# A DLRM tower on one core: the dot products of a tile issued in two parts instead of one

## The reference

```
e = stack([tbl_f[ids[:, f]] for f in range(27)], axis=1)     # [2048, 27, 128]
dot = einsum('bnd,bmd->bnm', e, e)
z = the 351 entries of dot with n < m, per sample
h = concatenate([z, dense_ctx], axis=1)                      # [2048, 367]
h = maximum(h @ W_top1 + b_top1, 0)                          # 512
h = maximum(h @ W_top2 + b_top2, 0)                          # 256
y = h @ W_top3                                               # [2048, 1]
```

## Time and profile before

| | before |
|---|---|
| runs, us | 588.22, 588.62, 590.11 |
| the profiled execution, us | 590.46 |
| its span, first to last instruction, us | 588.6 |
| mean granted TensorE clock, share of 2.4 GHz | 0.794 |
| TensorE matmul busy, us | 399.7 (68%) |
| GpSimd busy, us | 270.0 (46%) |
| VectorE busy, us | 248.6 (42%) |
| ScalarE busy, us | 163.6 (28%) |
| DMA, GB/s over the span | 62 |

### The profile page before, as it was taken

How to read it: one execution, slowest core, us unless ns; L and a number is a source line. 1 busy time by engine, 2 the same in 40 slices (tenths; PEclk the granted TensorE clock), 3 DMA queues, 4 the chain that set the end, 5 groups by cost and what they waited for, 6 DMA issues and landing times.

```text
span 588.6 us, 13981 instructions
## 1 busy us (share of the span) xinstructions
PE 399.7 (68%) x6083; PEld 360.4 (61%) x6083; DVE 248.6 (42%) x770; ACT 163.6 (28%) x217; POOL 270.0 (46%) x286
## 2 busy tenths in 40 slices
PE   4520176657595876949687685948778487969776
PEld 3420156557484775838586574938667476959665
DVE  5500224636244462506544262625635163647112
ACT  3210223314233222412324031422223132334241
POOL 6777462627446252645526164453536264530000
PEclk9855586958588686968879597887878697989898
DMA  8932130445213121321213022221213122210000
GB/s 196 246 87 59 35 79 20 111 126 139 55 46 72 29 72 29 71 52 50 68 30 82 22 64 57 51 73 29 73 38 77 34 55 69 54 34 2 2 2 2
DMA packets 23004, 36.65 MB, mean 62 GB/s; under 512 B 6224, under 2 KB 17120, under 8 KB 22944
## 3 DMA queue, kind: packets, MB, share of 16 engines
q0 software_dynamic: 8896, 18.24, 12.8%
q1 hardware_dynamic: 14048, 17.52, 11.8%
HBM read 35.73 MB, written 0.01 MB: 61 GB/s over the span
## 4 chain that ended last, share of the span: by engine, by line
PE 61%; issue 19%; another core or an unknown queue 9%; ACT 5%; DVE 2%; DMA 2%; SPq 1%; ACTq 0%; DVEq 0%
PE embT_ps L371 29%; PE gram_ps L397 12%; PE h_ps L426 7%; PE h_ps L450 5%; PE embT_ps L381 4%; ACT embT L575 2%; PE flat_ps L409 2%; PE embT_ps L366 2%; DMA embT<-in_tbl 2%; ACT embT L567 2%; DVE one_hot L493 2%; ACT tbl L555 1%; SPq L290 1%; SPq L282 0%
## 5 line engine op out<-in xcount | busy, mean ns | idle before, releaser
L340 POOL DMA_INDIRECT emb<-in_tbl,idx x272 | 263.5, 969 | 249.5 <-PE embT_ps L381 153.8
L371 PE MATMUL embT_ps<-one_hot,tbl 125*128 125x256 f32 x1284 | 214.1, 328 | 52.7 <-DVE one_hot L493 28.2
L493 DVE TENSOR_SCALAR one_hot<-ids,row_of 125x256 fp32r<-125x256 int32 x658 | 197.3, 371 | 108.9 <-PE embT_ps L371 47.9
L371 PEld LDWEIGHTS embT_ps<-one_hot,tbl 125*128 125x128 f32 x1284 | 195.5, 228 | 62.7 <-issue 30.7
L397 PE MATMUL gram_ps<-embT 128*27 128x27 f32 x4096 | 72.8, 217 | 97.5 <-issue 90.0
L397 PEld LDWEIGHTS gram_ps<-embT 128*27 128x27 f32 x4096 | 58.5, 129 | 113.4 <-issue 104.1
L567 ACT COPY embT<-embT_ps 128x256 f32<-128x256 f32 x77 | 52.1, 677 | 227.6 <-PE embT_ps L371 161.7
L575 ACT COPY embT<-embT_ps 128x512 f32<-128x512 f32 (+1 forms) x80 | 87.0, 1091 | 19.9 <-PE embT_ps L381 10.9
L521 DVE STREAM_TRANSPOSE flat<-gram_ps 128x864 f32<-128x864 f32 x16 | 17.3, 1083 | 169.2 <-PE gram_ps L397 169.2
L381 PE MATMUL embT_ps<-ident,emb 128*128 128x128 f32 x272 | 46.5, 288 | 29.8 <-ACT embT L567 22.4
L381 PEld LDWEIGHTS embT_ps<-ident,emb 128*128 128x128 f32 x272 | 34.3, 149 | 31.5 <-issue 31.0
(11 more groups left out here) (38 smaller groups left out, 75.1 us busy)
## 6 DMA issues: line engine op xcount, KB each, us to landing
ids<-in_ids_hot SPq DMA_DIRECT2D x77, 128.0 KB
emb<-in_tbl,idx POOLq DMA_INDIRECT x272
embT<-in_tbl SPq DMA_DIRECT2D x5, 448.0 KB
w_sb<-in_tbl SPq DMA_DIRECT2D x3, 560.0 KB
w_sb<-in_W_ring SPq DMA_DIRECT2D x1, 756.0 KB
w_sb<-in_W_top SPq DMA_DIRECT2D x1, 512.0 KB
h1T<-in_tbl SPq DMA_DIRECT2D x1, 448.0 KB
w_sb<-in_tbl SPq DMA_DIRECT2D x1, 448.0 KB
```

The lines of the kernel that those rows point to most:

```text
L340: pool.indirect_dma_start(gathered_row(t, s), None, tables[f][:, :], bass.IndirectOffsetOnAxis(ap=idx[:, t, f:f + 1], axis=0),).then_inc(g ...
L371: mm = pe.matmul(out[:, 0:HN], tbl[0:ROWS, part, AT[o] + chunk, :], one_hot[0:ROWS, k % SLOTS, c, :], start=(chunk == 0 and part == 0), st ...
L493: done = dve.tensor_scalar(one_hot[0:ROWS, k % SLOTS, c, :], of, row_of[0:ROWS, KINDS.index(CH[o]), chunk:chunk + 1], None, ALU.is_equal)
```

## The change

The dots of tile t - 1 are issued as two steps in a middle tile: groups 0 to 15 (64 samples) behind quad 0, where all were, and groups 16 to 31 behind quad 2. In the last tile the second part stands behind quad 0 of that tile, with a layer one between the parts. For the dots of the last tile itself, a layer two stands between the parts. VectorE's fill goes where the second part is.

```diff
@@ plan(t)
-            dots = [[("dots", t - 1, 0, GROUPS32)]]
+            dots = [[("dots", t - 1, 0, GROUPS32 // 2)], [], [("dots", t - 1, GROUPS32 // 2, GROUPS32)]]
...
-            return [("flat", t - 2), *dots[0], ("layer1", t - 3), ("quad", t, 0), ("layer1", t - 2),
+            return [("flat", t - 2), *dots[0], ("layer1", t - 3), ("quad", t, 0), *dots[2], ("layer1", t - 2),
                     ("quad", t, 1), ("layer2", t - 3), ("quad", t, 2), ("ring", t - 1), ("flat", t - 1),
                     ("layer2", t - 2), ("quad", t, 3), ("layer1", t - 1), ("quad", t, 4)]
...
-    END = [("dots", T - 1, 0, GROUPS32), ("layer2", T - 2), ("ring", T - 1), ("flat", T - 1), ("layer1", T - 1),
+    END = [("dots", T - 1, 0, GROUPS32 // 2), ("layer2", T - 2), ("dots", T - 1, GROUPS32 // 2, GROUPS32), ("ring", T - 1), ("flat", T - 1), ("layer1", T - 1),
            ("layer2", T - 1)]
```

## The result

| | before | after |
|---|---|---|
| runs, us | 588.22, 588.62, 590.11, 596.67 | 631.61, 632.13, 632.84, 636.47 |
| median, us | 589.37 | 632.49 |
| span of the profiled execution, us | 588.6 | 629.8 |
| mean granted clock | 0.794 | 0.805 |

The ratio is 1.0717, 95% interval 1.0618 to 1.0815: slower by 43 us, where 626 us was forecast, +37 on the median of before. That is the answer for the chip on which both ran. On another chip the same two kernels came out the other way round (0.9286), and what goes with that is the main thing that the experiments found.

A forecast was written before the change was run, and what follows sets the result against it. Gathers being issued on GpSimd were taken to slow TensorE's dots. Terms 3.6 + 1.3 - 1.8 = +3.1 us per tile, x 13 = +40, less 2.4 at the last tile, gave 626 us; 8-in-10 range 576 to 655, forecast's own 603 to 650.

The forecast's parts named there:

- What bounds the dots: In the dots' windows: while GpSimd issues gathers, 5 to 7 pairs pass per us; otherwise about 13.5 ns each.
- rival (a): Slowness belongs to quad 0, not gathers, so the part behind quad 2 takes 1.7 us; 562 us in all, chance 0.07.
- First part (A): 64 samples behind quad 0: slow stretch unchanged at about 7.7 us, then 1.0 us instead of 4.6; gain 3.6 per tile.
- Second part (B): 64 samples behind quad 2: slowed by eight gathers for 6.6 us, 7.2 us in all; bounds 5.7 and 10.
- Dots together: Both parts of a middle tile's dots: +7.2 - 3.6 = +3.6 us per tile, bounds -0.4 and +7.7.
- The hole: 1.84 us idle in the dots' fast stretch, read as TensorE outrunning instruction fetch; gone with parts of 128 pairs.
- rival (c): The idle hole stays in one of the parts: +24 us on the sum, 650 us, chance 0.07.
- The clock: Behind the second part the clock falls again: layer slower by 1.3 us per tile, bounds 0 and +1.7; mean under 0.79.
- Stalls: TensorE's stalls from quad 3 to next quad 0, 2.7 us on average: 1.8 per tile gone, bounds 0 and 2.7.
- At the end: Last tile: both parts run without gathers and the hole goes, -2.4 us; behind its own dots 0, bounds -2 and +3.6.
- the second slow block: Sign in a middle tile: L397 behind the third quad, few pairs per us until 1 to 2 us after the last gather.
- the wait "L397 <- issue": Sign: TensorE's idle time ahead of the dots' matmuls at over 130 us in place of 90.0.

The follow-up runs named there:

- Nogather: The kernel before and the changed kernel, each with the gathers of tiles 2 to 15 left out: 444.5 us and 391.8 us.
- hold: The kernel before and the changed kernel, each with GpSimd made to wait for dots before issuing certain gathers: 553.1 us and 532.3 us.
- around_table: Kernel before with dots of tiles 1 to 14 halved around quad 0's first table, ahead of quad 1; second-kind chip: 383.9 us against 417.9.
- hold_before: Kernel before, with GpSimd waiting ahead of quad 0's gathers of tile t + 2 for the dots behind quad 0: 553.1 us, 0.9408.
- hold_after: Changed kernel, with GpSimd waiting for the first part ahead of quad 0's gathers and the second ahead of quad 2's: 532.3 us, 0.9063 of kernel before.
- around_table_again: The around_table kernel unedited, on a chip of the first kind: 562.5 us against 585.1 for the kernel before, 0.9599.
- after_again: The changed kernel unedited, on a chip of the second kind: 384.7 us against 416.8 for the kernel before, 0.9286.
- behind_table: Kernel before with all dots in one block behind quad 0's first table in tiles 1 to 14; second-kind chip: 424.9 us against 417.9.
- nogather_before: Kernel before with the gathers of tiles 2 to 15 left out, on a chip of the first kind: 444.5 us, 0.7563.

## Why the prediction was right, and where it was off

**What bounds the dots**: right for this chip. Nogather, hold and around_table each take the gathers away from the dots in another way, and where no gather is in issue the slow stretch is gone. In hold_before the dots keep their place behind quad 0, so the place isn't the cause, and rival (a) is out. On the first kind (the changed kernel, hold_after and around_table_again) the length of a part of 128 pairs goes by the gathers that start or run in it: with two 4.0 to 4.9 us, with four 6.1 to 7.1, with six 9.8 to 10.9, with eight 12.1. The rate I had misread: 5 to 7 pairs per us after the first burst should have been 2.3 to 4.9 in the two tiles of the earlier trace rows (21 pairs in 4.3 us, 20 in 8.5). What I had taken for a rule of the kernel is one of the kernel and the chip, though: on the second kind parts with two or three gathers take 1.5 to 2.6 us (one of 57 takes 3.3). Nothing in the one trace that I had could show that, and with a trace of the other kind the forecast's own terms (no slow B, no hole) would have given a gain.

**First part (A)**: forecast no change in the slow part, 1.0 us for the rest. From the end of quad 0 it now ends after 2.2 and 9.9 us, 6.0 on average, where I had 7.7 + 1.0 = 8.7. I missed that one A in two would run at full speed. The reason is in GpSimd's and VectorE's timelines:

```profile
224.72 7.06 POOL L340 DMA_INDIRECT emb<-in_tbl,idx  x1 [9.40 <-PE embT_ps L381]
232.08 0.94 POOL L340 DMA_INDIRECT emb<-in_tbl,idx  x1 [0.30 <-issue]
```

```profile
222.46 8.49 DVE L493 TENSOR_SCALAR one_hot<-ids,row_of 125x256 fp32r<-125x256 int32 x32
```

One gather took 7.06 us, beside 32 one-hot builds in a row on VectorE that ended 0.83 us before it, and with no gather coming through, A took 1.8 us. The same stands in all five pairs from there on, and hold_after has four gathers of 5.9 to 6.8 us. The Trainium skill ("SBUF — State Buffer", SBUF: two separate sides) says that VectorE in certain modes holds a port that GpSimd needs to write descriptors. It fits this row, but elsewhere gathers ran beside builds at full speed: five beside 24 builds in a row in the kernel before (from 281.09 us, 0.94 to 0.96 us each), eight or nine beside 32 in a row in after_again (0.94 to 1.09). No run here isolated it, so this cause is argued and not shown.

**Second part (B)**: right in mechanism, the mis-sized term. 7.2 us was forecast, with bounds of 5.7 and 10; 11.4 (over my bound) and 8.8 were measured, 10.1 on average, and 10.1 over all 13 tiles too. I had let GpSimd reach quad 2 with four gathers to go. In the tile with the long gather it arrives with seven or eight, as what it was held up with is still to come. In the other tile its last gather ends 6.9 us after quad 2, where I had 6.2.

Dots together: forecast +3.6 us per tile, measured (1.80 + 11.39 + 9.97 + 8.81 - 23.4)/2 = +4.3, where 23.4 is the two blocks of the same pair before (9.73 and 13.64). A's miss and B's nearly cancel. Over all 13 tiles it is more, 16.3 us of parts against blocks of 11.0, +5.3, as the first four tiles have no fast part; the split of the loss below holds for this pair.

**The hole**: right. None of the 28 middle parts has one in its fast stretch (two slow stretches hold one idle time of 1.82 us among their shorter ones), and rival (c) is out. That it comes from the fetch of instructions is supported by one more trace. In behind_table the 3 matmuls of flat and the 16 of the table stand ahead of the dots, and in the eighth block the hole comes after 199 pairs, where it came after 219 (the rows of nogather_before above):

```profile
218.47 2.72 PE L397 MATMUL gram_ps<-embT 128*27 128x27 f32 x199
223.39 0.90 PE L397 MATMUL gram_ps<-embT 128*27 128x27 f32 x57 [2.20 <-issue]
```

In all 16 blocks of the two runs it stands within one matmul of the same place in the program, mostly 377 matmuls after the last one, though the dots begin elsewhere, and on a chip of the other kind. So it belongs to a place in the instruction stream and not to the dots. How many pairs in a row can pass without one wasn't measured.

**The clock**: forecast +1.3 us per tile behind B. The layers there took 3.93 and 3.23 us against 2.76 and 1.89 warm, +1.25 per tile. But behind A the table took 2.16 and 2.86 us, against 3.42 and 3.64 before, 1.0 back. The mean clock, which I had falling below 0.79, rose to 0.805. That sign of mine failed.

**Stalls**: from quad 3 to quad 0, 9.88 us became 5.34 (299.13 to 304.47) and 5.83 became 4.38: -3.0 us per tile, where I had -1.8 and at most -2.7. A new one appeared: quad 1 to quad 2 in the tile with layer ones takes 10.25 us (234.26 to 244.51) in place of 4.95, with 2.05 us on "issue" and a layer one of 4.27, while GpSimd issues what it was held up with: +2.65 per tile. The granted clock was 0.65 in that layer. What the layer waited for is a copy on ScalarE:

```profile
236.38 0.48 ACT L587 COPY flatT<-flat_ps 126x384 f32<-126x384 f32 x1 [4.58 <-remote]
```

It needs only TensorE's transposes of flat, which ended at 232.51, 3.9 us earlier. In this kernel that delay is 3.9 to 5.3 us in five tiles, where a long gather has just ended, and 0.04 us in nearly all others; in all 16 tiles of the kernel before it is 0.04. So with gathers in issue TensorE's results can reach another engine late, and not only the dots are slow. I had that effect in the stretch behind quad 3 and no term for it here. The waits behind quad 0 for ScalarE shrank by 0.6 per tile.

**Sum**: +4.3 + 1.25 - 1.0 - 3.0 + 2.65 - 0.6 = +3.6 us per tile, and 75.3 against 68.1 per pair is +3.6; forecast +3.1. At the end, from flat in the last tile to the last transpose, 36.2 us in place of 39.4: -3.3, forecast -2.4. So the mechanism and the sign are right, and that the size is too is in part luck: its terms miss both ways. Of the signs that I named, the second slow block, the missing hole and the clock's fall behind B came; the wait "L397 <- issue" stopped just short of 130 us (129.2), and the mean clock rose.

## What to carry to other kernels

Look at how long a stream of many short instructions takes against what other queues are issuing, not only against its own waits: here, on chips of the first kind, moving a piece of it to just behind the step that releases gathers cost 43 us, and holding the gathers back or moving the piece ahead of the release gained 23 to 55 us with the same work. Split such a stream into short parts (128 pairs were short enough here, 256 weren't), and put each part where nothing has just been released. And time a change on more than one chip before believing its sign.

## What the runs showed of the hardware that I had not expected

The same kernel took 585 to 587 us on three chips, and 589 in the comparison of the result, and 417 to 418 on two. The change was 7% slower on the one chip of the first kind that ran it and about 7% faster on the one of the second. The visible difference is that on the first kind TensorE idles between bursts of a few short matmuls while gathers are issued, 2 to 8 pairs per us behind the first burst; a gather mostly takes 0.94 us and a build 0.36 to 0.38 on average on both. What sets the chips apart stays open.

A hole, mostly of 1 to 3 us (0.8 to 3.8), stood in nearly every run of 256 short weight-load and matmul pairs, on both kinds and at the same place in the program. Of the parts of 128 one had such a hole, of 1.74 us, in around_table on the second kind (at 73.13 us, with a table and another part just ahead of it).

A single gather can take 7.06 us in place of 0.94, in the changed kernel once per pair of tiles, at the same place each time.
